# Which unit of a head's turned squares ScalarE empties: the second instead of the third, in the loop of a transformer expert layer

## What is computed

```python
def _expert(x, Wqkv, bqkv, Wo, bo, g1, be1, W1, bf1, W2, bf2, g2, be2):
    q, k, v = jnp.split(x @ Wqkv.T + bqkv, 3, axis=-1)             # 8 heads of 32 features
    attn = softmax(einsum('bhqd,bhkd->bhqk', q * scale, k))        # over all 1354 tokens
    ctx = einsum('bhqk,bhkd->bhqd', attn, v) @ Wo.T + bo
    x = _layernorm(x + ctx, g1, be1)
    h = gelu(x @ W1.T + bf1)
    h = gelu(h @ W2.T + bf2)
    return _layernorm(x + h, g2, be2)
```

## Time and profile before

| | |
|---|---|
| median of 3 runs | 3402.9 us (3399.01 to 3406.57) |
| the profiled execution's own time | 3405.69 us |
| its span (first to last instruction) | 3403.9 us |
| mean granted TensorE clock | 0.878 of full speed |
| PE busy, matmuls | 2668.7 us, 78% of the span |
| DVE busy | 1654.8 us, 49% |
| ACT busy | 1115.8 us, 33% |
| the loop changed here, first score matmul to last `mix` | 1786.0 to 2929.9 us |

### The profile page before, as it was taken

The page is one execution under the profiler, slowest core; times in us unless marked ns, Lnnn a source line. Parts: engine busy times, 40 slices in busy tenths (PEclk is TensorE's granted clock), DMA queues, the critical chain, the costliest instruction groups (busy, mean ns, idle before and its releaser), DMA issues. The chain is left out here.

```text
span 3403.9 us, 53143 instructions
## 1 busy us (share of the span) xinstructions
PE 2668.7 (78%) x18883; PEld 2132.7 (63%) x18883; DVE 1654.8 (49%) x3220; ACT 1115.8 (33%) x2110; POOL 493.6 (14%) x758
## 2 busy tenths in 40 slices
PE   6988598599778589965848888888888888734795
PEld 4868598599457344454846677777777777524453
DVE  3636321322247312333427777777777777342353
ACT  2323121122123110001205555555555555223242
POOL 0000122122021000000000111111111111100077
PEclk9989699599689689976979999999999999757797
DMA  4000122244131010021770411442353521120100
GB/s 115 1 7 1 54 87 63 76 126 121 46 91 50 26 56 0 9 41 70 275 256 28 110 59 36 114 115 69 105 134 98 144 75 33 38 50 1 41 25 26
DMA packets 122568, 243.95 MB, mean 72 GB/s; under 512 B 30040, under 2 KB 69682, under 8 KB 118480
## 3 DMA queue, kind: packets, MB, share of 16 engines
q1 hardware_dynamic: 108592, 203.06, 19.2%
q0 software_dynamic: 13728, 37.64, 4.5%
HBM read 451.99 MB, written 53.98 MB: 149 GB/s over the span
## 5 line engine op out<-in xcount | busy, mean ns | idle before, releaser
L2224 PE MATMUL tx_ring<-g_ident,tx_p 128*128 128x128 f32 x2552 | 426.4, 298 | 129.4 <-issue 45.5
L2224 PEld LDWEIGHTS tx_ring<-g_ident,tx_p 128*128 128x128 f32 x2552 | 313.7, 151 | 224.3 <-issue 63.2
L2442 DVE TENSOR_REDUCE tx_neg_max<-tx_scores 128x1 f32<-128x1354 f32 x232 | 362.1, 1561 | 45.4 <-PE tx_scores L2212 45.4
L2449 DVE COPY tx_p_t<-tx_ring 128x512 f32<-128x512 f32 x464 | 306.8, 687 | 134.5 <-PE tx_ring L2224 129.1
L2349 ACT ACTIVATE tx_p<-tx_scores,tx_neg_max 128x1354 f32<-128x1354 f32 x232 | 322.6, 1390 | 96.2 <-DVE tx_neg_max L2442 95.9
L2212 PE MATMUL tx_scores<-tx_keys,tx_queries 96*128 96x512 f32 (+1 forms) x696 | 221.7, 431 | 30.6 <-DMA tx_queries<-tx_q_hi 30.6
L2356 ACT ACTIVATE tx_p_t<-tx_ring 128x384 f32<-128x384 f32 x232 | 113.6, 490 | 356.1 <-PE tx_ring L2224 355.1
L2263 PE MATMUL tx_ring<-tx_p_t,tx_values 128*32 128x128 f32 x5104 | 153.2, 276 | 21.2 <-ACT tx_p_t L2356 20.8
L1297 PE MATMUL sro_ring<-sro_we,sr_h 128*128 128x512 f32 x352 | 155.8, 601 | 6.1 <-DMA sro_we<-_L_ffn_expert_out_weight 6.1
L2263 PEld LDWEIGHTS tx_ring<-tx_p_t,tx_values 128*32 128x32 f32 x5104 | 137.3, 111 | 35.4 <-ACT tx_p_t L2356 34.4
L2212 PEld LDWEIGHTS tx_scores<-tx_keys,tx_queries 96*128 96x128 f32 x696 | 127.7, 212 | 43.2 <-issue 31.0
(11 more groups left out here) (759 smaller groups left out, 5464.9 us busy)
## 6 DMA issues: line engine op xcount, KB each, us to landing
tx_keys<-expert_keys SPq DMA_DIRECT2D x696, 169.5 KB
lv1e_w<-in_L_ffn_W SPq DMA_DIRECT2D x232, 256.0 KB
tx_w<-in_L_ffn_W SPq DMA_DIRECT2D x58, 1024.0 KB
lv0e_w<-in_L_ffn_W SPq DMA_DIRECT2D x200, 256.0 KB
tx_values<-expert_values SPq DMA_DIRECT2D x58, 704.0 KB
tx_rows<-in_L_ffn_rows SPq DMA_DIRECT2D x29, 640.0 KB
g_adj_t<-in_adj_t POOLq DMA_DIRECT2D x4, 3872.0 KB, 22.9
expert_values<-kv_v SPq DMA_DIRECT2D x8, 1408.0 KB, 5.7
```

Of the source, the lines that this page charges most:

```text
L2224: last = nc.tensor.transpose(ring[u % 2][:, (t - t0) * P:(t - t0 + 1) * P], p[n % 2][:, t * P:(t + 1) * P], g.ident[:])
L2442: nc.vector.tensor_reduce(neg_max[:, n % 4:n % 4 + 1], sc[n % 2][:, 0:N], AX_X, ALU.max, negate=True)\
L2449: nc.vector.tensor_copy(p_t[:, n % TURNED, t0:t0 + nt, :], ring[u % 2][:, 0:nt * P].rearrange("p (t q) -> p t q", q=P))\
```

## The change

The engines of units 1 and 2 of each head are exchanged: ACT empties unit 1 (four squares, 128x512) and DVE units 0 and 2 (128x512 and three squares, 128x384). The place of the copies in the two orders stays: on DVE both come ahead of `row_max`, on ACT the one copy comes behind `exponent` of the next head. PE's instructions and their order are the same.

```diff
     for kind, _, part in order:
-        eng = ("act" if part[1] == 2 else "dve") if kind == "heads" else drained_by[kind]
+        eng = ("act" if part[1] == 1 else "dve") if kind == "heads" else drained_by[kind]
         counts[eng] += 1
...
             def keep_turned(i, hd):
-                u, n = at["heads", i, (hd, 2)], HEADS * i + hd
-                t0, nt = TG[2]
+                u, n = at["heads", i, (hd, 1)], HEADS * i + hd
+                t0, nt = TG[1]
                 act.wait_ge(full, u + 1)
...
                     if i < tiles:
                         keep_turned(i, hd, 0)
-                        keep_turned(i, hd, 1)
+                        keep_turned(i, hd, 2)
                         if HEADS * i + hd + AHEAD < heads:
                             row_max(HEADS * i + hd + AHEAD)
```

## The result

The changed kernel takes 3524.3 us, median of four runs (3495.1 to 3538.6), against 3403.7 (3399.0 to 3406.6): 1.0345 times, with an interval of 1.0273 to 1.0416. It is slower, as forecast, but by 121 us and not by 42, above the range's end of 3482. The profiled execution is the fastest of the four: 3495.07 us with a span of 3493.3, 89 us above the profiled one of before. The mean granted clock was 0.865 in it and 0.846, 0.846 and 0.857 in the other three, 0.878 before.

What follows compares the result with a forecast made beforehand. The prediction took a chain through PE, DVE and ACT with little slack to bound the loop. Lateness of 1.5 us per tile over 28 passages gave 42 us on 3403 us: 3445 us, range 3411 to 3482.

Steps and rivals of the forecast that it cites:

- Durations of the copies: Per head: DVE's copy of 512 at 0.687 us becomes 384 at about 0.558; ACT's 0.490 becomes 0.598.
- Wait (a): DVE's maximum of head n+2 stands behind the copy of unit 2, turned after the scores: 0.72 us late at head 1.
- the sum: Lateness of DVE and PE carried forward head by head through one tile of the earlier trace, about 1.5 us per tile.
- Wait (b): Unit 0 of the next head needs unit 1's bank, freed by ACT 1.39 + 0.65 us after the exponentials' start.
- Head 3 … Head 4 begins at 2232.04 against 2230.47, +1.57: Head 3's query work and first copy follow the late maximum; its own maximum is +2.14 us, head 4's start +1.57.
- `mix` waits for it … +1.03: At head 4 `mix` waits for DVE's small copy: 2235.77 against 2234.74, 1.03 us late.
- That is 1.5 us per tile: Total lateness per tile of the expert loop; over 28 passages between tiles, 42 us.
- Rival 3: PE's clock falls more often: one more 1.1 us stretch per tile, 31 us on top, 3476 us; 12%.
- Where DVE is late anyway, a slow stretch costs nothing more: Remark within the rival on PE's clock: low-clock stretches add no time where DVE is already late; no size given.
- Rival 1: DVE is relieved of 30 us of copying and that decides: faster, 3373 us; 8%.
- Rival 2: Lateness mostly absorbed under `mix` and the layers: +8 to +25 us, 3411 to 3428 us; 12%.
- What would show it: List of expected signs: copy times, later maximum, new PE and DVE waits, 1.5 us longer tile, and what would refute it.

## Why the prediction was right and wrong

- **Durations of the copies**: right. 558 ns for 384 on DVE as read from the earlier trace rows, 593 on ACT for 598.
- **Wait (a)**: right in place and size. At head 1 the maximum begins 0.47 behind the small copy (0.50 taken) and the turns of head 2 are +0.70 (0.72); behind head 6 the maximum is 0.80 later relative to the exponentials of head 7 (2227.37 and 2226.82, before 2245.93 and 2246.18), where the sum has 1.65 less 0.83, 0.82.
- **Wait (b)**: right: 1.39 + 0.63 behind the exponentials (0.65 taken).
- **"Head 3 … Head 4 begins at 2232.04 against 2230.47, +1.57"**: wrong. Counted from unit 2 of head 1, unit 2 of head 3 was +0.55 and head 4 began at +0.62, in tiles with full clock there. The cast of the queries, 0.85 us in the row before, took 0.29 now: it began 0.17 ahead of GpSimd's operation (2250.02 and 2250.19 above) and not behind its begin. I had carried its duration along as a constant.
- **"`mix` waits for it … +1.03"**: +1.33 measured between tiles at full clock there. The walked tile had `mix` 14.14 us behind unit 2 of head 1, a tile at full clock 12.87: the clock was low from 2230.9 on, in its heads 3 and 4, which hid lateness. The cast's 0.56 went the other way, so the two errors partly cancel. I should have chosen a tile at full clock for the walk.
- **"That is 1.5 us per tile"**: 1.8 at full clock, 49 us for 42. By itself this would have given 3453, inside the range.
- **Rival 3, "PE's clock falls more often … 1.1 us for one such stretch. One more in every tile"**: this is the step that failed. In the sum itself the change of the clock stood at nothing, as if the clock were a property of the kernel and not of where its waits lie. The rival had the mechanism and gave it 12%, but its term was too small, 1.1 us a tile, 31 us. One stretch did cost 1.1 (40.96 less 39.86). But the long tiles have slow turns, second layer and `mix`, and lose 4.5 us against a mean of 1.5 before. Of the 121 us between the medians some 72 are left to the clock.
- **The Trainium skill**, TensorE: Matmul & The Clock Gate, "What's actually happening", ties the clock to how busy PE has been. Stretches at 0.50 do follow waits here, and a late DVE brought more of them (0.92 granted for 0.95). Yet 10 of 25 tiles before had the same waits and no such stretch, and the added products (slower on the kernel before, faster on the changed one) do not move the time in one direction, so the size could not be had from it.
- **"Where DVE is late anyway, a slow stretch costs nothing more"**: borne out in part. With the reduction added on DVE the clock was lower and cost 1.2 us a tile instead of 1.5. It did not help the change, whose slow stretches also cover the second layer and `mix`.
- **Rival 1**, DVE relieved: refuted. DVE lost 39 us of work and the kernel 121 us. **Rival 2**, absorbed: holds at heads 0 and 5 only.
- **"What would show it"** had "I am wrong if … the granted clock in the loop differs and accounts for the time". That came true for more than half of it.

Open: what tips the clock from one pattern into another within one program (40.96 to 44.37 us at 2343 to 2470 us) is not settled. The runs show that it does, and that shifts under 2 us in a tile move it either way. The length of the tile alone is not it: the change and the change with the GELU moved both have 39.9 us at full clock, and were granted 0.90 and 0.95. The full-clock tile of heads 6 and 7, and wait (a) entirely by itself, were not measured.

## What to carry to other kernels

Before two engines exchange a copy, look at what stands behind it in each queue: the relieved engine can become the late one, because it now waits for its input ahead of work that others need. Measure such edits on stretches of equal granted clock, and price the clock apart: in this loop, with waits of 1 to 2 us on PE, edits of a few tenths of a us moved the total by one to two per cent either way. It is then worth trying neighbours of the schedule. A wait added on one engine can shorten another on PE, as it did at head 3; read every wait of the tile again before you call an edit harmless.

## What the hardware showed that I had not expected

- One program has two steady lengths of the same tile, 40.96 us at 0.96 and 44.37 at 0.85. Its four runs, granted 0.846 to 0.865 in the mean, spread by 1.2%; those of the kernel before spread by 0.2% beside them and by up to 0.5% elsewhere.
- A wait added on DVE made the kernel 1.0% faster (3368.5 for 3401.2), 0.4 us of added products per tile made the changed one 1.3% faster (3477.9 for 3524.3).
- DVE's cast of 128x256 to fp32r took about 0.85 us where it began some 0.03 us behind a GpSimd operation on the same size, in 26 of 29 tiles before. Where it began 0.17 ahead of one it took 0.29, though the two overlap for 0.12, in 27 of 29 tiles with the change and in the kernel before with the wait alone. Why it began sooner is not shown. Before, DVE and POOL in the timeline:

```profile
2226.89 0.85 DVE L2464 CAST tx_q_hi<-tx_q 128x256 fp32r<-128x256 f32 x1
...
2226.86 0.73 POOL L2601 TENSOR_TENSOR tx_x_r<-tx_x_n,tx_rows 128x256 f32<-128x256 f32 x1 [2.27 <-DVE tx_x_n L2503]
```
